# Down weights stored as halves and loaded by chunk pairs, sums of step one held, low passes of down in two waits

## The reference

```python
x = layernorm(x + attention(x))          # x: 4 batches x 1024 tokens x 512
x = layernorm(x + ffn(x))
def ffn(x):                               # 512 -> 2048 -> 512
    x = fwht(x * SU_ug) / 64
    up   = x @ W_up.T   * (scale_ug[:2048] * 64)
    gate = x @ W_gate.T * (scale_ug[2048:] * 64)
    h = fwht(silu(gate) * up * SU_dp) / 64
    return h @ W_down.T * (scale_dp * 64)
```

## Time and profile before

| | us |
|---|---|
| median of three runs | 1555.61 |
| the profiled execution | 1557.91 |
| its span, first to last instruction | 1556.1 |
| TensorE busy | 1522.9 |
| VectorE busy | 1035.8 |
| ScalarE busy | 625.6 |
| GpSimd busy | 466.1 |

### The profile page before, as it was taken

The page is one execution under the profiler, slowest core; times in us unless marked ns, Lnnn a source line. Parts: engine busy times, 40 slices in busy tenths (PEclk is TensorE's granted clock), DMA queues, the critical chain, the costliest instruction groups (busy, mean ns, idle before and its releaser), DMA issues.

```text
span 1556.1 us, 26452 instructions
## 1 busy us (share of the span) xinstructions
PE 1522.9 (98%) x10152; PEld 1365.6 (88%) x10152; DVE 1035.8 (67%) x1790; ACT 625.6 (40%) x1289; POOL 466.1 (30%) x580
## 2 busy tenths in 40 slices
PE   6999999999999999999999999999999999999998
PEld 5977978888887888899999999999999999999997
DVE  6876786687678986864575576475566457557545
ACT  4163255236227665533333333333343334333322
POOL 5465456447438434500300130030030031003001
PEclk9999999999999999999999999999999999999999
DMA  7031122122122796677668668677767867766862
GB/s 283 1 108 76 35 82 102 35 82 102 64 77 93 286 380 256 245 263 282 231 243 290 236 211 292 226 243 255 269 225 236 292 216 255 277 231 220 282 225 95
DMA packets 92060, 307.44 MB, mean 198 GB/s; under 512 B 9888, under 2 KB 10272, under 8 KB 90144
## 3 DMA queue, kind: packets, MB, share of 16 engines
q1 hardware_dynamic: 90928, 301.54, 54.9%
q10 hardware_dynamic: 1008, 4.20, 0.7%
HBM read 255.37 MB, written 50.33 MB: 196 GB/s over the span
## 4 chain that ended last, share of the span: by engine, by line
PE 63%; DVE 5%; ACT 1%; issue 1%; POOL 1%; POOLq 0%; DVEq 0%; ACTq 0%
PE ff_bank_b L2058 16%; PE ff_bank_a L2058 11%; PE ff_bank_c L2058 11%; PE ff_acc L2085 7%; PE ff_acc L2086 7%; PE ff_acc L2078 7%; DVE ff_d_lo L1775 2%; PE ff_x_ps L2009 1%; PE ff_x_ps L2029 1%; ACT at_union L601 1%; DVE ff_h_lo L1794 1%; DVE ff_c L1826 0%; PE ff_x_ps L2017 0%; PE ff_x_ps L2018 0%; DVE ff_ring L1770 0%
## 5 line engine op out<-in xcount | busy, mean ns | idle before, releaser
L2058 PE MATMUL ff_bank_b<-ff_x_hi,ff_ring 128*128 128x256 f32 x1536 | 302.2, 280 | 2.5 <-DVE ff_c L1826 1.9
L2058 PEld LDWEIGHTS ff_bank_b<-ff_x_hi,ff_ring 128*128 128x128 f32 x1536 | 247.8, 188 | 3.8 <-issue 3.7
L2058 PE MATMUL ff_bank_b<-ff_x_lo,ff_ring 128*128 128x256 f32 x768 | 214.2, 279 | 0.0
L2058 PE MATMUL ff_bank_c<-ff_x_hi,ff_ring 128*128 128x256 f32 x1024 | 203.9, 282 | 0.0
L2058 PE MATMUL ff_bank_a<-ff_x_hi,ff_ring 128*128 128x256 f32 x1024 | 203.4, 282 | 0.0
L2085 PE MATMUL ff_acc<-ff_d_lo,ff_h_hi 128*128 128x512 f32 x504 | 198.0, 393 | 1.3 <-DVE ff_d_lo L1775 1.3
L2086 PE MATMUL ff_acc<-ff_d_hi,ff_h_lo 128*128 128x512 f32 x504 | 196.1, 389 | 0.0
L2058 PEld LDWEIGHTS ff_bank_a<-ff_x_hi,ff_ring 128*128 128x128 f32 x1024 | 165.3, 188 | 2.7 <-issue 0.2
L2058 PEld LDWEIGHTS ff_bank_c<-ff_x_hi,ff_ring 128*128 128x128 f32 x1024 | 165.1, 188 | 2.3 <-issue 2.3
L1822 DVE TENSOR_TENSOR ff_c<-ff_bank_b,ff_c 128x512 f32<-128x512 f32 x64 | 44.3, 692 | 175.3 <-PE ff_bank_b L2058 174.0
L2058 PEld LDWEIGHTS ff_bank_b<-ff_x_lo,ff_ring 128*128 128x128 f32 x768 | 143.7, 187 | 0.0
(11 more groups left out here) (323 smaller groups left out, 3471.2 us busy)
## 6 DMA issues: line engine op xcount, KB each, us to landing
ff_ring<-gu_scratch SPq DMA_DIRECT2D x392, 512.0 KB, 4.9
gu_scratch<-ff_ring SPq DMA_DIRECT2D x56, 512.0 KB, 4.4
at_xt<-in_xt SPq DMA_DIRECT2D x4, 2048.0 KB, 8.4
at_xn<-in_x SPq DMA_DIRECT2D x32, 256.0 KB, 2.9
x_scratch<-at_x SPq DMA_DIRECT2D x32, 256.0 KB, 2.0
ff_raw<-in_wgu SPq DMA_DIRECT2D x8, 1024.0 KB, 7.8
at_wd_a<-in_wd SPq DMA_DIRECT2D x8, 512.0 KB, 4.7
mixed_scratch<-at_wd_a SPq DMA_DIRECT2D x8, 512.0 KB, 3.2
```

The source lines that it names most:

```text
L2058: i = pe.matmul(bank[:, m, :], r[:, a, m, c, :], b[:, k, c, :], start=(k < 3 and m == 0 and c == 0 and b is x_hi and a == 0), stop=(m == 1 ...
```

## The change

Down weights: the scaling of piece 0 goes from VectorE to GpSimd. ScalarE rounds each scaled piece (`round_down`) into `wd_b`, GpSimd lowers it (`lower_down`) in place in `wd_a`, and SP stores both halves, so that there are 16 stores of 512 KB and the DRAM buffer is twice as large. The mix in the FFN is then two fp32r matmuls, one for each half, with `hr`, the rounded matrix, instead of one of f32. Instead of two transfers of 2 MB at the start of the FFN there are four of 512 KB (pairs 0 and 1), and two more for pair p + 1 at the first product store of step p, for p = 1 to 6, once the two mixes of each step before have been made. The chunks' buffer is split in two of the same total size. The y fetch for block 1 goes from product 7 to product 17.

Sums: GpSimd's `run` begins with a wait for the third split of x of block 0, so that the sums of step one start after it. Down: `h_lo` by `d_hi` for all, then the wait for `d_lo`, then `h_hi` by `d_lo`.

```diff
                         sp.wait_ge(wo_lo_s, 1)
-                    sp.wait_ge(*(wd_out.now(b, 16) if k else wd_out.last(b, 32)))
+                    sp.wait_ge(*(wd_out.now(b, 32) if k else wd_out.last(b, 64)))
                     sp.dma_start(wd_a[:, :, :], io["wd"][b * 2 + k]).then_inc(wd_in.sem, 16)
                 def store_down(k):
-                    sp.wait_ge(*wd_mixed.now(b, 9 * k + 9))
-                    sp.dma_start(mixed_dram[b * 2 + k], wd_a[:, :, :]).then_inc(wd_out.sem, 16)
+                    sp.wait_ge(*wd_mixed.now(b, 11 * k + 10))
+                    sp.dma_start(mixed_dram[b * 2 + k, 0], wd_b[:, :, :]).then_inc(wd_out.sem, 16)
+                    sp.wait_ge(*wd_mixed.now(b, 11 * k + 11))
+                    sp.dma_start(mixed_dram[b * 2 + k, 1], wd_a[:, :, :]).then_inc(wd_out.sem, 16)
                 load_down(0)
...
                     sp.dma_start(x1_dram[b, t], x1[:, t % 2, :]).then_inc(x1_out[t % 2].sem, 16)
+                store_down(0)
                 for t in range(TILES):
                     if t == TILES - 1 and not fetch:
-                        return lambda: store(t)
+                        return lambda: store(t), lambda: store_down(1)
                     store(t)
...
                     if t == 0:
-                        store_down(0)
-                    if t == 1:
                         load_down(1)
-                    if t == RT:
+                    if fetch and t == RT:
                         store_down(1)
...
             sp.dma_start(held["y0"][:, :, :], first_x1).then_inc(held_in[1], 16)
-            last_store = tiles(B - 1, False)
+            last_store, last_down = tiles(B - 1, False)
             ahead.store_first()
-            sp.wait_ge(*wd_out.now(B - 1, 32))
+            last_down()
+            sp.wait_ge(*wd_out.now(B - 1, 64))
             sp.wait_ge(*out_ps.now(B - 1, TILES))
...
                 else:
-                    pool.wait_ge(*wd_mixed.now(b, 10 * k + 2 * stage))
+                    pool.wait_ge(*wd_mixed.now(b, 12 * k + 2 * stage))
                 pool.tensor_tensor(pair(dst)[:, :, 0], pair(src)[:, :, 0], pair(src)[:, :, 1], ALU.add).then_inc(wd_mixed.sem, 1)
                 pool.tensor_tensor(pair(dst)[:, :, 1], pair(src)[:, :, 0], pair(src)[:, :, 1], ALU.subtract).then_inc(wd_mixed.sem, 1)
+
+            def scale_down(b):
+
+                pool.wait_ge(held_in[0], 16)
+                pool.wait_ge(*wd_mixed.now(b, 8))
+                for h in range(2):
+                    v = wd_a[:, IC // 2 * h:IC // 2 * h + IC // 2, :]
+                    i = pool.tensor_tensor(v, v, bc(held["dps"][:, 2 * WC * b:2 * WC * b + WC], 1, IC // 2), ALU.mult)
+                i.then_inc(wd_mixed.sem, 1)
+
+            def lower_down(b, k):
+
+                pool.wait_ge(*wd_mixed.now(b, 11 * k + 10))
+                pool.tensor_tensor(wd_a[:, :, :].bitcast(F32R), wd_a[:, :, :], wd_b[:, :, :], ALU.subtract).then_inc(wd_mixed.sem, 1)
             def batch(b, more):
...
                 mix_down(b, 0, 3)
+                scale_down(b)
                 split_x(b, 3)
+                lower_down(b, 0)
                 for t in range(RT - 2):
...
                     split_x(b + 1, 1)
-                else:
+                lower_down(b, 1)
+                if not more:
                     return lambda: inverse_deviation(b, TILES - 1)
...
                 act.activation(q_hi[tt], flat(big[:, 2 * tt:2 * tt + 2, :]).rearrange("p (c q) -> p c q", q=P), ACT.Copy).then_inc(qt_hi_s.sem, 1)
+
+            def round_down(b, k):
+                act.wait_ge(*wd_mixed.now(b, 11 * k + 9))
+                act.activation(wd_b[:, :, :].bitcast(F32R), wd_a[:, :, :], ACT.Copy).then_inc(wd_mixed.sem, 1)
             def batch(b, more):
...
                 split_x(b, 3)
+                round_down(b, 0)
                 def local_exponentials(i, pairs=(0, 1)):
...
                     if i == 9 and not more:
+                        round_down(b, 1)
                         ahead.first_mixed()
...
                     return lambda: scale_x1(b, TILES - 1)
+                round_down(b, 1)
                 scale_x1(b, TILES - 1)
...
                     dve.tensor_tensor(vwo_lo[:, a, :], (acc, tr)[a][0:HK, :], vwo_hi[:, a, :].bitcast(F32), ALU.subtract).then_inc(vwo_lo_s.sem, 1)
-                def scale_down(k, halves):
-
-                    n = 2 * b + k
-                    dve.wait_ge(*(wd_in.now(b, 32) if k else wd_mixed.now(b, 8)))
+                def scale_down():
+
+                    dve.wait_ge(*wd_in.now(b, 32))
                     dve.wait_ge(held_in[0], 16)
-                    for h in halves:
+                    dve.wait_ge(*wd_mixed.now(b, 11))
+                    for h in range(2):
                         v = wd_a[:, IC // 2 * h:IC // 2 * h + IC // 2, :]
-                        i = dve.tensor_tensor(v, v, bc(held["dps"][:, WC * n:WC * n + WC], 1, IC // 2), ALU.mult)
-                    if halves[-1]:
-                        i.then_inc(wd_mixed.sem, 1)
+                        i = dve.tensor_tensor(v, v, bc(held["dps"][:, WC * (2 * b + 1):WC * (2 * b + 2)], 1, IC // 2), ALU.mult)
+                    i.then_inc(wd_mixed.sem, 1)
                 def softmax_in(t):
...
                         transposed_queries(0)
-                        scale_down(1, (0, 1))
+                        scale_down()
                         local_maxima(0)
-                    if t in (2, 3):
-                        scale_down(0, (t - 2,))
                     if t >= 1:
...
         sb, ps, signal, sem = tools(nc, ctx, sems, "ff")
-        wd = sb("wd", [P, WP, IC, WC])
+        down_in = [sb(f"down_in{i}", [P, 2, WP, 2, WC], F32R) for i in range(2)]
+        wd_first = sb("wd_first", [P, WP, IC // 2, WC])
         hr, hr_minus = sb("hr", [P, P], F32R), sb("hr_minus", [P, P], F32R)
...
         rstd = sb("rstd", [P, 2, FT])
+        wd_second = sb("wd_second", [P, WP, IC // 2, WC])
         acc = ps("acc", [P, FT, 512])
...
         def down_chunk(i):
-            return wd[:, :, i, :]
+            return (wd_first, wd_second)[i // 8][:, :, i % 8, :]
         def by_piece(t):
...
                 sp.dma_start(raw[pair % 2][:, :, :], io["wgu"][pair]).then_inc(raw_in[pair % 2], 16)
-            def down_weights(n):
-                half = slice(IC // 2 * n, IC // 2 * n + IC // 2)
-                sp.dma_start(wd[:, :, half, :], mixed_dram[:, :, half, :].rearrange("w p i n -> p w i n")).then_inc(wd_in[n], 16)
+            def down_weights(pair):
+                if pair >= 2:
+                    sp.wait_ge(w_had, 2 * pair - 2)
+                for h in range(2):
+                    sp.dma_start(down_in[pair % 2][:, h].bitcast(F32),
+                                 mixed_dram[:, h, :, 2 * pair:2 * pair + 2, :].rearrange("w p i n -> p w i n")).then_inc(wd_in[pair % 2], 16)
             def store_product(n):
...
                             finish()
+                        if n == 2 * MULS + 3:
                             fetch(1, 0, 1)
...
                             weights(p + 2)
+                        if k == 0 and 2 <= p + 1 < PAIRS:
+                            down_weights(p + 1)
                     for n in range(PRODUCTS - RING, PRODUCTS):
...
             def run(close_attention):
+                pool.wait_ge(*x_lo_s.now(0, 3))
                 for p in range(1, PAIRS - 1):
...
             def mix_down(i, turned, hadamarded):
-                pe.wait_ge(wd_in[i // 8], 16)
+                pe.wait_ge(wd_in[i // 2 % 2], 32 * (i // 4 + 1))
                 if i:
...
                 pe.wait_ge(*xm_s.now(1, hadamarded))
-                pe.matmul(x_ps[:, :], had[:, :], down_chunk(i), start=True, stop=True).then_inc(w_had, 1)
+                chunk = down_in[i // 2 % 2]
+                pe.matmul(x_ps[:, :], hr[:, :], chunk[:, 0, :, i % 2, :], start=True, stop=False)
+                pe.matmul(x_ps[:, :], hr[:, :], chunk[:, 1, :, i % 2, :], start=False, stop=True).then_inc(w_had, 1)
             def multiply(s, blk, p, k, first):
...
                 pe.wait_ge(*h_lo_s.now(s, 2))
+                for j in range(2):
+                    for t in range(FT):
+                        k = slice(P * t, P * t + P)
+                        pe.matmul(acc[:, t, :], h_lo[q][:, j, k], d_hi[:, j, :], start=False, stop=False)
                 pe.wait_ge(*d_lo_s.now(s, 1))
...
                         k = slice(P * t, P * t + P)
-                        pe.matmul(acc[:, t, :], h_hi[q][:, j, k], d_lo[:, j, :], start=False, stop=False)
-                        i = pe.matmul(acc[:, t, :], h_lo[q][:, j, k], d_hi[:, j, :], start=False, stop=last and j == 1)
+                        i = pe.matmul(acc[:, t, :], h_hi[q][:, j, k], d_lo[:, j, :], start=False, stop=last and j == 1)
                 i.then_inc(down_s.sem, 1)
...
     x1_dram = nc.dram_tensor("x1_scratch", [B * T, D], F32, kind="Internal").ap()
```

(2 more changed lines are left out.)

2 lines of the change are left out of this document (1 added, 1 removed).

## The result

The changed kernel is slower: 1561.56 us against 1556.18 us (medians of 8 runs each), a ratio of 1.0031 with a 95% interval from 1.0022 to 1.0041, or +4.8 us (the two medians lie 5.4 us apart; I go by the ratio throughout). The forecast was 1551.9 us, with a range from 1547.3 to 1557.5 us. The profiled execution of the changed kernel took 1561.65 us, with a span of 1559.8 us, 3.7 us more than the profiled one of before.

What follows compares the result with a forecast made beforehand. TensorE, busy 1522.9 of 1556.1 us, was taken as the bound. Start +1.8, mixes -0.4, -0.8, -2.8 and -0.8, low-weight waits -0.7 made -3.7 us: 1555.6 to 1551.9 us, range 1547.3 to 1557.5 us.

Steps and rivals of the forecast that it cites:

- held sums and two waits in down: First FFN block: moved sums make VectorE 2.3 us late; waits for low down weights that go count 0.7 us gained.
- mixes, net of what waits take: First FFN block: 16 mixes, each about 0.4 us shorter, 6.2 us if TensorE is never held there; some gains swallowed.
- I take 0; bounds -0.5 and +3.6 us: FFN down-weight loads: at most 4.8 us of transfer work a step, offset by the later y fetch, so no cost.
- Rival B: FFN steps 2 to 4: added loads delay ring stores, ScalarE and mix 4; +7.2 us, 1559.1 us; chance 0.09.
- the 5 us it had named: Sign in the FFN: ScalarE's longest waits for a ring slot should stay under 5 us, else B.
- I take 0 per batch: Attention's four batches: the lowering beside the softmax fits its slack, cost 0; bounds 0.5 us better, 1.6 us worse.
- I take 1.0: Near 512 us: with sums moved, TensorE's 0.97 us wait for the probabilities' low half goes, gaining 1.0 us.
- 3.3 us had been forecast: Block 0, near 520 us: about three VectorE operations held 1.1 us each beside GpSimd's sums, 3.3 us in all.
- rival A: Start of the FFN: held sums do not collide where it matters; start -1.8 us, 1548.3 us; chance 0.22.
- third mix's 0.4 us: FFN block 0's start: the third mix is 0.4 us shorter, and that counts in full.
- no price for the second wait in down: The 63 downs: one more wait amid the low passes costs 0, at most 2.5 us.
- the swallowed gain in step 6: FFN step 6: mix 13's gain is eaten, as mix 14 waits 0.93 us for a fold behind VectorE's slow chain.

Runs made afterwards that it cites:

- e10: Kernel before with the changed attention alone; the FFN loads only the high half in two transfers, f32 mixes, sums not held, one wait in down: 1.0019, +3.0 us.
- e9: e4's kernel with each mix one f32 matmul again, low halves left out: 1.0012 of the kernel before.
- e4: Changed kernel, but only the high half, loaded by two 2 MB transfers at the FFN's start and used twice, y fetch at product 7: 0.9983.
- e1: Changed kernel with down halves laid out by chunk pairs, so the FFN's loads read 4 KB rows: 1.0015 of the kernel before.
- e6: Changed kernel with 4 KB rows in the down loads and the y fetch back at product 7: 1.0007 of the kernel before.
- e16: e10 with GpSimd's lowering of piece 0 waiting for the first pooled softmax: 1.0018 of the kernel before.
- e15: e10 with GpSimd's lowering in attention cut to one element: 1.0000 of the kernel before.
- e8: Kernel before with the two waits in down alone: 1.0000 of the kernel before.
- e7: Kernel before with GpSimd's wait for the third split of x alone: 1.0010, +1.6 us.
- e3: Changed kernel without GpSimd's wait for the third split of x: 1.0036 of the kernel before.

## Why the prediction was wrong

The experiments make a ledger (each difference of two about ±2 us, e10 alone ±1.4 us). It adds up to the measured +4.8 us because each row begins at the run at which the one before ends, so the sum is no check of the single rows:

| part | forecast | measured | from |
|---|---|---|---|
| attention's part | 0 | +3.0 | e10 |
| held sums and two waits in down | +1.6 (2.3 - 0.7) | -1.1 | e9 less e10 |
| mixes, net of what waits take | -5.3 | -4.5 | e4 less e9 |
| how the halves are loaded | 0 | +7.5 | changed kernel less e4 |

- **The step that failed is "I take 0; bounds -0.5 and +3.6 us" for the transfers.** It measured +7.5 us, twice the bound. Its working compared landing times of transfers (2.4 us for 512 KB in short rows against 2.7 us in long ones), the short ones taken from two small loads. By its own rows 0.3 us for 56 KB make 2.7 us and not 2.4 us for 512 KB, so no advantage of the short rows either. What counted was the stretch in which the share was already 1.00 in the same group of rows: there each transfer added keeps SyncE in its issue, and all behind it is late. By the ratios 2.5 us of it are the short rows (e1), 1.2 us come with the early y fetch once the rows are long (e6 less e1), and 3.7 us are the additional bytes and transfers of each step (e6 less e4). By the traces from the first mix on it is 4.6, 0.4 and 2.1 us. The sum is firm, its division is not, and the part of the y fetch cannot be told from nothing.
- **Rival B had the mechanism, not the place, and the amount by luck.** B's +7.2 us (above the forecast's own bound of +3.6 us for B) were 2.4 us in each of three steps; the measured 7.5 us are mostly one wait and the clock after it. It looked at ring stores and mix 4. Its sign did come: ScalarE's longest wait for a ring slot was 6.49 us (at 546.91 us), above the 5 us it had named, but mix 4 did not wait. The raw weights two steps ahead stand last in SyncE's order of a step, so they collect all delays, and the first turn of x waits for a fold behind the ScalarE operation that reads them. B priced the wait alone; after it TensorE at half clock cost 2.8 us more. Its chance of 0.09 was too low for a stretch with the share at 1.00.
- **"I take 0 per batch" for attention failed as well.** The working looked at the softmax, where e16 finds nothing. The lowering costs 3.0 us all the same, since e15 gives them back. What the working missed is that at the end of the last batch GpSimd's program has the lowering ahead of the sums. In e10 what collides there is not the lowering itself but what it pushed; that this makes most of the 3.0 us is likely, not shown (e15, e16).
- **"I take 1.0" for the held sums' old place was wrong in its cause.** e8 and e10 lose the wait without the hold. The new place was right: two differences of x took 2.39 us, and a split 1.77 us, beside GpSimd, and the second mix stood 2.2 us later against the start of block 0 (14.37 us in the changed kernel, 12.15 us before), where 3.3 us had been forecast before the 1.0 us was taken off. VectorE and GpSimd in the changed kernel:

```profile
518.17 2.39 DVE L1999 TENSOR_TENSOR ff_xm<-ff_xm 128x512 f32<-128x512 f32 x2
520.49 1.77 DVE L1797 TENSOR_TENSOR ff_x_lo<-ff_xm,ff_x_hi 128x512 fp32r<-128x512 f32 x1
...
518.33 1.68 POOL L1520 TENSOR_TENSOR ff_sums<-ff_raw 128x512 f32<-128x512 f32 x1 [6.31 <-DVE ff_x_lo L1797]
520.09 1.62 POOL L1523 TENSOR_TENSOR ff_sums<-ff_sums,ff_raw 128x512 f32<-128x512 f32 x1
```

  The Trainium skill ("GPSIMD Engine Reference", section Specifications) names just this contention, and these rows agree. So rival A falls. Alone the hold costs 1.6 us (e7). Behind the new lowering it may pay, since the sums collide without it as well (e3, e9 less e10), but both differences, 0.8 and 1.1 us, are within their intervals.
- **The gain of the mixes in steps 0 and 1 was not there.** The forecast counted the third mix's 0.4 us as gained. From mix 2 to mix 3 the changed kernel takes 10.84 us against 9.86 us before, because TensorE comes to bank b before VectorE has evicted it (e9).
- **Right:** 0.46 us for a mix; blocks 1 to 7 unchanged (from mix 15 to the end 901.5 us before, 901.3 us in the changed kernel, whose mix 15 is 0.4 us shorter); no price for the second wait in down; the swallowed gain in step 6. There the changed kernel waits 1.54 us for VectorE and 0.93 us at mix 14, so 1.0 us rather than 0.4 us of the mixes' gain is lost.
- **The Trainium skill** ("DMA: Bandwidth & Descriptors", section Specifications) has 512 bytes as enough for line rate. Here the loads at the start moved 300 GB/s in 512-byte rows (share 1.16) and 391 GB/s in 4 KB rows (share 1.00, e1). The measurement decides: at 512 bytes the rate was below that of longer rows.

## What to carry to other kernels

Price a transfer where it will be issued: where the queues' share is already 1.00, what was added here delayed what stood last in the issuing engine's order, so look up who waits for that one and what clock TensorE has after the wait. Keep rows long on the side that is read in the full stretch, and pay for the short ones where the queues idle. When an operation is added to an in-order engine, look also at what it pushes, and take a wait seen in one execution at a near-tie of two engines for a draw until a second trace shows it.
